# One 2048-wide exponential for two heads in place of two 1024-wide ones, in the attention stage of a fused transformer layer

## What is computed

```python
xn = _layernorm(x)
# attention, 32 query heads, 8 key/value heads, head size 128, rotary positions, causal
scores = jnp.einsum('bhqd,bhkd->bhqk', q, k) / math.sqrt(D)
scores = jnp.where(causal, scores, -1e9)
attn = jax.nn.softmax(scores, axis=-1)
s = jnp.einsum('bhqk,bhkd->bqhd', attn, v) @ Wo.T      # after a reshape
g = _silu(_L0_ffn_ref(xn, A, B, Wr))   # top 2 of 4 low-rank experts, rank 16
x = x + s * g
```

## Time and profile before

| | us |
|---|---|
| median of the 3 runs | 4317.05 |
| lowest and highest | 4140.98, 4496.07 |
| the profiled execution | 4071.24 |
| its span, core 2, the slowest | 4069.7 |
| PE busy in the span | 3533.8 (87%) |
| ACT busy | 1227.0 (30%) |
| DVE busy | 797.4 (20%) |

### The profile page before, as it was taken

The page is one execution under the profiler, slowest core; times in us unless marked ns, Lnnn a source line. Parts: engine busy times, 40 slices in busy tenths (PEclk is TensorE's granted clock), DMA queues, the critical chain, the costliest instruction groups (busy, mean ns, idle before and its releaser), DMA issues.

```text
span 4069.7 us, 41671 instructions; the slowest of 8 cores (4041.6 to 4069.7 us)
## 1 busy us (share of the span) xinstructions
PE 3533.8 (87%) x15444; PEld 1380.5 (34%) x15444; DVE 797.4 (20%) x1643; ACT 1227.0 (30%) x1488; POOL 97.5 (2%) x152
## 2 busy tenths in 40 slices
PE   1488999996688999995878878888888999999998
PEld 0233444442333444442221212221222444444443
DVE  3400111112400111111222222222222111111111
ACT  2200111121200111113777776776775000000000
POOL 0000000000000000000000000000000000000000
PEclk9689999998699999997888988997998999999999
DMA  6632444483632554442010010000000434343432
GB/s 66 65 65 39 89 94 95 90 123 51 73 65 40 95 94 93 91 91 67 11 29 24 11 29 24 11 27 25 15 14 32 110 108 114 103 118 99 119 99 78
DMA packets 163301, 273.41 MB, mean 67 GB/s; under 512 B 106336, under 2 KB 122848, under 8 KB 142432
## 3 DMA queue, kind: packets, MB, share of 16 engines
q0 software_dynamic: 84736, 152.23, 24.3%
q1 hardware_dynamic: 78368, 118.52, 8.2%
HBM read 364.22 MB, written 58.72 MB: 104 GB/s over the span
## 4 chain that ended last, share of the span: by engine, by line
PE 80%; ACT 9%; issue 4%; DMA 3%; DVE 3%; ACTq 0%; SPq 0%; DVEq 0%; POOLq 0%
PE sqp L608 27%; PE stp L887 22%; PE otp L792 7%; PE denrb L802 7%; PE svp L466 6%; PE ptp L753 6%; ACT pt L770 3%; ACT pt L763 2%; DMA xsq<-xT 2%; PE prp L365 1%; ACT recf L826 1%; DMA qt<-QTs 1%; ACT xsq L356 1%; PE dlp L894 1%; PE rotp L618 1%
## 5 line engine op out<-in xcount | busy, mean ns | idle before, releaser
L608 PE MATMUL sqp<-xnT,wg 128*128 128x512 bf16 x5120 | 1122.1, 380 | 3.3 <-DVE mid_sb L585 3.3
L887 PE MATMUL stp<-OTr,wo 128*128 128x512 bf16 x4096 | 897.7, 380 | 2.2 <-DVE OTr L839 2.2
L608 PEld LDWEIGHTS sqp<-xnT,wg 128*128 128x128 bf16 x5120 | 501.6, 98 | 611.0 <-issue 10.8
L887 PEld LDWEIGHTS stp<-OTr,wo 128*128 128x128 bf16 x4096 | 396.1, 98 | 499.5 <-issue 32.8
L753 PE MATMUL ptp<-qt,ktg 128*128 128x512 bf16 (+3 forms) x1280 | 343.4, 380 | 166.2 <-DMA qt<-QTs 61.7
L763 ACT ACTIVATE pt<-ptp,cf_sb 128x1024 bf16<-128x1024 f32 x384 | 438.5, 1194 | 117.8 <-PE ptp L753 116.6
L792 PE MATMUL otp<-pt,vg 128*128 128x512 bf16 (+3 forms) x1280 | 384.7, 386 | 10.0 <-DVE pt L778 9.0
L611 ACT CAST qraw<-sqp 128x1024 bf16<-128x1024 f32 x80 | 81.0, 1012 | 1029.4 <-PE sqp L608 979.0
L802 PE MATMUL denrb<-pt,const_sb 128*1 128x512 bf16 (+3 forms) x1280 | 367.5, 371 | 0.0
L770 ACT ACTIVATE pt<-ptp,cf_sb 128x512 bf16<-128x512 f32 (+3 forms) x512 | 295.3, 614 | 134.4 <-PE ptp L753 109.8
L898 ACT ACTIVATE gt<-dlp 128x1024 bf16<-128x1024 f32 x64 | 65.5, 1024 | 844.9 <-PE dlp L894 844.9
(11 more groups left out here) (103 smaller groups left out, 1258.5 us busy)
## 6 DMA issues: line engine op xcount, KB each, us to landing
wg<-Wblk POOLq DMA_DIRECT2D x96, 1024.0 KB, 8.6
wo<-Wo_blk POOLq DMA_DIRECT2D x32, 1024.0 KB, 9.1
xt<-xT SPq DMA_DIRECT2D x32, 1024.0 KB, 8.4
outT<-outst SPq DMA_DIRECT2D x64, 512.0 KB, 4.2
xsq<-xT POOLq DMA_DIRECT2D x16, 1024.0 KB, 20.2
QTs<-qsp SPq DMA_DIRECT2D x64, 256.0 KB, 5.3
qt<-QTs SPq DMA_DIRECT2D x128, 128.0 KB, 2.3
Vs<-vstag SPq DMA_DIRECT2D x16, 256.0 KB, 5.1
```

The lines of the kernel that those rows point to most:

```text
L608: t.matmul(o, l, r, start=st, stop=sp),
L887: t.matmul(o, l, r, start=st, stop=sp),
```

## The change

The four slots of exponentials become slices of one SBUF tensor `ptsb_t`, and the two score buffers slices of one PSUM tensor `ptp_t`, so that each pair of neighbours is one contiguous range. In a full step the two calls of `rec_exp` are replaced by one ACTIVATE over 2048 columns, which reads both score buffers and writes both slots. In a diagonal step the calls are as before. Scores and the matmuls of `rec_pv` are recorded as before.

```diff
-            pt_sb = [p2.enter_context(nc.sbuf_tensor(f"pt{i}", [128, 2 * TT], BF16)) for i in range(4)]
+            ptsb_t = p2.enter_context(nc.sbuf_tensor("ptsb", [128, 8 * TT], BF16))
+            pt_sb = [ptsb_t[:, 2 * TT * i:2 * TT * (i + 1)] for i in range(4)]
...
-            pt_ps = [p2.enter_context(nc.psum_tensor(f"ptp{i}", [128, 2 * TT], F32)) for i in range(2)]
+            ptp_t = p2.enter_context(nc.psum_tensor("ptp", [128, 4 * TT], F32))
+            pt_ps = [ptp_t[:, 0:2 * TT], ptp_t[:, 2 * TT:4 * TT]]
...
                             while pending_tail:
                                 pending_tail.pop(0)()
-                            rec_exp(j, 0, slot_of(j, 0))
-                            rec_exp(j, 1, slot_of(j, 1))
+                            vis_j = [max(0, (2 * j + half) * 128 - t0) for half in range(2)]
+                            if vis_j[0] == 0 and vis_j[1] == 0:
+                                sA = slot_of(j, 0)
+                                sch.op("sc", lambda s,
+                                       o=ptsb_t[:, sA * 2 * TT: sA * 2 * TT + 4 * TT],
+                                       i=ptp_t[:, 0:4 * TT]:
+                                       s.activation(o, i, AF.Exp, bias=SHIFT_c, scale=ISD_c),
+                                       reads=[b_ptps[0], b_ptps[1], b_cf],
+                                       writes=[b_ptsb[sA], b_ptsb[sA + 1]])
+                            else:
+                                rec_exp(j, 0, slot_of(j, 0))
+                                rec_exp(j, 1, slot_of(j, 1))
```

## The result

| | before | after |
|---|---|---|
| runs at full speed, us | 4062 to 4070 | 4160 to 4165 |
| ratio to before | | 1.0238, 95% interval 1.022 to 1.0255 |
| median of all runs, us | 4160.95 (10 runs) | 4236.25 (8 runs) |
| attention stage on core 2, us | 1224.7 | 1324.4 |
| at 1.2 GHz in that stage, us | 296 | 433 |

The change makes the kernel about 97 us slower. In some executions one die or both run slower at a lower granted clock, whatever the kernel; the ratios, the stretches shown and the attention stages compared here are from runs, cores or (in e6 and e7) stages that this left alone.

The account below looks back on a forecast made before the run. PE was taken to set attention's pace; 37.3 us in steady steps plus 19.3 at unit starts made 57 us, 4071.2 to 4128 us profiled (own range 4116 to 4146), or 4374 us for the runs (range 4120 to 4500).

Parts of the forecast that it names:

- The wide exponential: In full attention steps, one 2048-column exponential takes 2.04 us, against 2.30 for two of 1024 in a row.
- The serial loop: In later full steps, scores and exponential no longer overlap: period 3.373 us instead of 2.985; 96 steps, 37.3 us slower.
- s(1) 0.85 us later at each start: At 48 unit starts, step 1's four score matmuls begin 0.85 us later than their first half did, but whole.
- What step 1 gives back: At unit starts, a shorter step 1 leaves a net +0.37 us, or +0.59 at full clock; 19.3 us in all.
- left where it is: At unit starts, the 1.2 GHz stretch stays at about 2464.5 to 2467.9 despite the delay: +0.37 us in 41 starts.
- Rival 3: At unit starts, a second half-clock stretch may follow in half of them: 37 us, total 94; chance 0.10.
- Rival 4: In steady steps, PE's 0.39 us gaps bring half clock in a third of 96: +77, total 134 us; chance 0.06.
- Rival 1: In the attention loop, ACT's saving counts if ACT bounds it: 50 us gained, 4021 us; chance 0.04.
- Rival 2: At unit starts, the clock pays back: 63 us at most would cancel the loss, 4065 us; chance 0.06.
- Rival 5: In full steps the 2048-wide exponential takes near 2.30 us, or its starts are later: 4167 us; chance 0.12.
- Moves at no cost: Allocations, diagonal steps with their masks, and group changes waiting for the queries' DMA were each counted at zero.

Follow-up runs that it names:

- e6: Kernel before the change, two 1024-wide exponentials, head 0's score buffer held until the second exponential ends: ratio 1.0237 to before.
- e7: Kernel before the change, first exponential made to wait for both heads' scores, buffers still freed one at a time: ratio 1.0058 to before.
- e5: Kernel before the change, two 1024-wide exponentials, each waiting for both heads' scores and holding both score buffers: ratio 1.0289 to before.
- e3: Changed kernel, PE's waits at unit starts filled with repeated step-0 scores and 7 matmuls whose results are unused: 4060.32 and 4060.38 us.
- e1: Changed kernel, but step 0 keeps two 1024-wide exponentials; only full steps from 1 on use the 2048-wide one: ratio 1.0108 to before.
- e2: Changed kernel, but only step 0 of the 48 units beginning with a full step uses the 2048-wide exponential: ratio 1.0103 to before.
- e4: Kernel before the change, PE's waits at unit starts filled with repeated step-0 scores and 4 unused matmuls: 3981.95 us in one run.
- e8: Kernel before the change, only the later wait of each unit start filled, with 4 unused matmuls, scores not repeated: ratio 0.9855 to before.

## Why the prediction was wrong

- **The forecast** was +57 us on the scale of the profiled execution (4128 us), within 2%. It was +97 (4163), slower by 2.4%. The range for the runs' time, 4120 to 4500, held the median of 4236.25, but only because it was made wide for the runs' scatter, which is luck and not insight; the time given in it, 4374, took over the median of three scattered runs, and the ten runs of before now have their median at 4160.95. The forecast's own range, 4116 to 4146, missed.
- **The wide exponential**: 2.04 us was forecast, 2.052 measured over 192. Right. The Trainium skill (ScalarE: Activation LUTs, What ACT_TABLE_LOAD costs) gives the 1.99 us for an ACTIVATE with a pointer as bias, and 93 ns for each pointer operand. The prediction overlooked that this one has its scale by a pointer too (`ISD_c`). An estimate from the figures of that section for both pointers, 186 + 2 x 93 + 0.833 x 2048 ns, is 2.08 us; the 2.052 measured lies between, and the measurement decides.
- **The serial loop**: 3.373 us forecast, 3.38 measured; 96 steps cost 38.6 us, forecast 37.3. Right, and shown by e5 to e7: the joined waits alone make it 3.62, each alone 3.19.
- **s(1) 0.85 us later at each start**: right, 3.69 to 4.54 in most units (3.66 to 4.53 in the mean), 41.4 us over 48 starts.
- **What step 1 gives back**: this is the step that failed. With the half-clock stretch "left where it is" I let step 1 shrink, so that a start cost only +0.37, or +0.59 at full clock, 19.3 us in all. Step 1 grew from 4.73 to 5.13 us, and the starts cost 60.8. The stretch did not stay. In before 4 of 48 starts had a double stretch and 7 had none; in after 34 had a double one and none was spared. With the clock up, step 1 is 3.38 in after (e3) and 3.63 in before. So the half clock costs 48 x (4.73 - 3.63) = 53 us in before and 48 x (5.13 - 3.38) = 84 in after: +31. Without it the starts cost 30 us, close to the 28 that 48 x 0.59 gives. I had booked the clock as a gain of 9 us, and it was a loss of 31: that is the 40 us missing.
- **Rival 3**, more half clock at the starts, was the outcome, and had a chance of 0.10: 37 us were written for it, total 94, with "it decides from 16 starts on". That the total came so near is in part luck: 24 starts at 1.54 us were written. In after 30 more starts had a double stretch, but step 1 with a double one takes only 0.93 us more than with a single one (5.40 against 4.47, means of after), and none of the 7 starts spared in before was spared. The argument for the rival stood in the prediction: the wait before s(1) grows. What I left out is that the same wait goes with how soon the clock comes back: in the earlier trace rows PE's work resumed at 2463.07, before the half-clock stretch began at about 2464.5; in after it resumes at 2514.77, more than a microsecond after the clock fell (0.50 from 2513.4 on). The clock records of all 48 starts say the same. In the 34 with a double stretch in after, s(1) began 1.34 to 2.10 us after the fall; in the 14 with a single one, 0.69 us after it at the latest, or before it. In before it is 0.65 to 1.02 us in the 4 with a double one, and 0.46 at the latest in the 37.
- **Rival 4**, half clock in the steady steps, did not come: the clock is 1.00 there with a gap of 0.34 us in each loop. The Trainium skill (TensorE: Matmul & The Clock Gate, A second HAM failure mode: psum-queue depth-cycling) describes such short idles as a cause of a swinging clock; this trace disagrees for gaps of this size, and agrees at the starts, where PE waits 1.12 and then 1.57 us with one matmul between. e1 shows both in one kernel. **Rivals 1, 2 and 5** did not come either.
- **Moves at no cost**: the allocations, tile 0's units (170.3 to 171.1 us for all 16) and the group starts were rightly at zero.

What stays open: whether it is the place of s(1) against the clock's fall that makes a stretch single or double. The 14 starts of after, and the 26 of e2, that get a single one are those where s(1) came sooner after the fall, or before it (in e2 at most 0.80 us after it, against 0.85 or more with a double one). No run here moved a unit against the clock's changes by itself, so this is an order seen in the traces and not a test.

## What to carry to other kernels

Before merging two instructions that read double-buffered data, write down the loop that the joined waits close: here 0.25 us of fixed cost was saved and 0.65 us of overlap lost in each step, and the dearer of the two waits was the one that held the buffer. Where PE waits already lower its clock, a change that lengthens them must be priced with the clock, in before's own rows of both levels, and the case in which the low stretch grows deserves more than the 0.10 that it got here. A wait that can't be shortened can be filled: 7 or 8 matmuls of no use at most starts made this kernel 2% faster.

## What the runs showed of the hardware that I had not expected

- Matmuls whose results nobody reads keep the granted clock up: 0.88 to 0.97 in the stage with 8 more per start (e4), 0.84 to 0.97 with 11 (e3). Matmuls with a single output row (the denominator's, 128*1) serve for it: e8 adds nothing else, and its time at 1.2 GHz falls from 296 to 136 us.
- 0.85 us more of waiting at 48 places brought 137 us more at 1.2 GHz (296 to 433), far more than the waiting itself (41 us). What it cost was 31 us, less than half of what 137 us full of PE work at half speed would have cost (68): the rest fell on times when PE waited anyway.
- One ACTIVATE may read four PSUM banks at the usual rate: 2052 ns for 2048 columns, 858 ns more than for 1024.
